# Moving weight and quantization work between engines in a gated cross-attention and ternary-FFN kernel

## The reference

```
for each of 4 batch elements (512 tokens x 512 channels):
  h    = layernorm(layernorm(x)) with weights
  q, qx, k, v = fp8(h / in_scale) @ fp8 weights        # 16, 16, 8, 8 heads of 128
  kx, vx      = ctx @ w_kv_x                            # 8 heads each
  core = softmax(LN(q)  LN(k)^T  / sqrt(128)) v         # 2 q heads per k head
  xout = softmax(LN(qx) LN(kx)^T / sqrt(128)) vx
  x1   = x + tanh(g) * ( fp8(clip([core, xout] / smooth)) @ wproj ) * scales
  a, b = int8(layernorm(x1)) @ ternary(w_gate_up)
  out  = x1 + tanh(g2) * ( int8(silu(a) * b) @ ternary(w_down) )

ternary(w) = clip(round(w / mean|w|), -1, 1) * mean|w|
```

## Time and profile before

| | us |
|---|---|
| median of 3 runs (lowest, highest) | 1862.5 (1860.2, 1867.2) |
| the profiled execution | 1860.7 |
| its span, first to last instruction | 1858.9 |
| PE busy | 1629.7 |
| DVE busy | 1575.9 |
| ACT busy | 1350.9 |
| POOL busy | 1095.2 |

### The profile page before, as it was taken

How to read it: one execution, slowest core, us unless ns; L and a number is a source line. 1 busy time by engine, 2 the same in 40 slices (tenths; PEclk the granted TensorE clock), 3 DMA queues, 4 the chain that set the end, 5 groups by cost and what they waited for, 6 DMA issues and landing times.

```text
span 1858.9 us, 35181 instructions
## 1 busy us (share of the span) xinstructions
PE 1629.7 (88%) x11164; PEld 1007.7 (54%) x11164; DVE 1575.9 (85%) x3451; ACT 1350.9 (73%) x3351; POOL 1095.2 (59%) x1421
## 2 busy tenths in 40 slices
PE   2478899788999998899899888999999879999996
PEld 1355555455656665566566555666666434444442
DVE  7569899999898899988888999999988856777774
ACT  6468998777889987898898788998988842222222
POOL 3677888876776777776777667777767530000000
PEclk9889999999999999999999999999999989999997
DMA  3357899889999998899899998999999966322200
GB/s 101 96 149 168 190 192 211 174 187 193 203 226 202 194 224 180 191 208 249 192 207 200 229 193 195 233 231 222 217 232 181 205 157 214 105 69 80 69 18 17
DMA packets 669597, 325.48 MB, mean 175 GB/s; under 512 B 552288, under 2 KB 595424, under 8 KB 669152
## 3 DMA queue, kind: packets, MB, share of 16 engines
q1 hardware_dynamic: 669408, 323.17, 77.5%
HBM read 140.61 MB, written 48.23 MB: 102 GB/s over the span
## 4 chain that ended last, share of the span: by engine, by line
PE 41%; DVE 26%; POOL 12%; ACT 8%; issue 7%; DMA 4%; SPq 1%; ACTq 0%; DVEq 0%; POOLq 0%
PE psum L699 7%; PE psum L687 6%; PE psum L654 6%; PE psum L741 6%; PE psum L716 6%; DVE pp L981 5%; DVE nmx L971 5%; PE psum L661 3%; DMA pt<-pp 3%; PE psum L758 3%; PE psum L674 2%; POOL wbt L1513 2%; POOL qk L1566 2%; ACT pp L1330 1%; POOL ars L1544 1%
## 5 line engine op out<-in xcount | busy, mean ns | idle before, releaser
L687 PE MATMUL psum<-qk 128*128 128x512 f16 x1536 | 421.9, 384 | 29.0 <-DVE pp L981 22.9
L699 PE MATMUL psum<-pt,vv 128*128 128x512 f16 x1536 | 398.5, 382 | 55.8 <-ACT cy L1338 40.6
L654 PE MATMUL psum<-wbt,xqt 128*128 128x256 f16 (+1 forms) x4096 | 411.3, 251 | 25.1 <-DVE xqt L898 11.1
L654 PEld LDWEIGHTS psum<-wbt,xqt 128*128 128x128 f16 x4096 | 333.6, 100 | 135.5 <-issue 20.4
L1319 ACT ACTIVATE psum<-psum,nmx 128x512 f32<-128x512 f32 x512 | 344.4, 673 | 84.9 <-DVE nmx L971 80.4
L981 DVE SCALAR_TENSOR_TENSOR pp<-psum,prs,pp 128x512 f16<-128x512 f32 x512 | 378.5, 739 | 5.5 <-ACT pp L1330 5.2
L971 DVE TENSOR_REDUCE nmx<-psum 128x1 f32<-128x512 f32 x512 | 344.5, 673 | 36.7 <-PE psum L687 35.2
L1330 ACT ACTIVATE pp<-psum,prs 128x512 f16<-128x512 f32 x512 | 356.7, 697 | 18.5 <-DMA pt<-pp 18.2
L699 PEld LDWEIGHTS psum<-pt,vv 128*128 128x128 f16 x1536 | 147.5, 98 | 252.5 <-issue 70.0
L1566 POOL TENSOR_TENSOR qk<-y,qk 128x512 f16<-128x512 f32 x192 | 233.7, 1217 | 16.0
L687 PEld LDWEIGHTS psum<-qk 128*128 128x128 f16 x1536 | 143.8, 99 | 114.7 <-DVE pp L981 26.0
(11 more groups left out here) (176 smaller groups left out, 2711.1 us busy)
## 6 DMA issues: line engine op xcount, KB each, us to landing
wbt<-ws SPq DMA_DIRECT2D x192, 256.0 KB, 3.8
ws<-wbt SPq DMA_DIRECT2D x64, 256.0 KB, 4.0
catd<-cy SPq DMA_DIRECT2D x64, 256.0 KB, 3.3
raw<-in_wgu SPq DMA_DIRECT2D x64, 256.0 KB, 3.6
raw<-in_w SPq DMA_DIRECT2D x32, 384.0 KB, 3.7
wbt<-catd SPq DMA_DIRECT2D x6, 2048.0 KB, 9.8
pt<-pp SPq DMA_TRANSPOSE x512, 3.7
raw<-in_wp SPq DMA_DIRECT2D x32, 256.0 KB, 3.8
```

The lines of the kernel that those rows point to most:

```text
L654: ins = e.matmul(bank[:, o0:o0 + c1 - c0], xv[:, v, kt * 512 + tt * 128:kt * 512 + (tt + 1) * 128], wb[i][:, h, kt, c0:c1], start=kt == 0 ...
L687: ins = e.matmul(SB(n), qk[i][:, jq, u, ss], qk[i][:, jk, w, :], start=k == 0, stop=k == 2)
L699: ins = e.matmul(OB, v[:, t, u, att, :], src[:, w, t, :], start=t == 0 and k == 0, stop=t == 3 and k == 2)
```

## The change

Five edits, all in phase A: (1) the high part of a split job is made by ACT (`job_hi`, at slot n, behind ACT's other work) instead of POOL; (2) its low part by POOL at n+1 instead of DVE; (3) in a ternary job POOL clips the rounded value in place at n+1, to MAGIC - 1 and MAGIC + 1, and DVE only subtracts MAGIC, at n+2; (4) for batch elements 2 and 3 the clip of each input part is done by POOL in the same slot; (5) all output steps come one slot later. In slots modulo 16 the output clip moves from 1 and 9 to 2 and 10, the DVE steps from 2, 3, 4 and 10, 11, 12 to 3, 4, 5 and 11, 12, 13, the subtractions from 5, 7, 13, 15 to 6, 8, 14, 0.

```diff
-POOL_HI = 2
+POOL_HI, POOL_X = 2, 2
-OUT_AT = {"clip": 17, "field": 18, "step": 19, "add": 20, "sub": (21, 23), "store": 26}
+OUT_AT = {"clip": 18, "field": 19, "step": 20, "add": 21, "sub": (22, 24), "store": 27}
@@ DVE x_quant
+                if step == 0 and b >= POOL_X:
+                    return
@@ DVE job
-                if what == "tern":
-                    q.done(e.tensor_scalar(ob, f, MAGIC, 1.0, ALU.subtract, ALU.min))
-                    e.tensor_scalar(ob, ob, -1.0, None, ALU.max).then_inc(s["l_t2"], 1)
-                else:
-                    e.tensor_tensor(o.bitcast(F16)[:, 0:512], f, wps[:, j, :], ALU.subtract).then_inc(s["l_lo"], 1)
+                q.wait_ge("l_tc", JV["l_tc", m])
+                e.tensor_scalar(raw[i][:, 512:768].bitcast(BF16)[:, 0:512], raw[i][:, 0:512], MAGIC, None,
+                                ALU.subtract).then_inc(s["l_t2"], 1)
-                if JOB_AT.get(n - 1, -1) >= 0:
-                    job(JOB_AT[n - 1])
+                if JOB_AT.get(n - 2, -1) >= 0:
+                    job(JOB_AT[n - 2])
@@ ACT
+            def job_hi(m):
+                j, i = JOBS[m][2], (K0 + m) % 2
+                q.wait_ge(f"raw_ld{i}", JV[f"raw_ld{i}", K0 + m])
+                e.activation(wps[:, j, :], raw[i][:, 0:512], ACT.Copy).then_inc(s["l_hi"], 1)
@@ POOL
+            def x_clip(b, k):
+                part = k // 5
+                v, half_ = divmod(part, 2)
+                src = xq[b % 2][:, v, half_ * 1024:(half_ + 1) * 1024]
+                q.wait_ge("xy", xy_value(b, 3, v))
+                q.wait_ge("x_w", ((b - 1) * 8 + part) * 4)
+                e.tensor_scalar(src, src, 448.0, -448.0, ALU.min, ALU.max).then_inc(s["x_w"], 1)
@@ POOL job (now called at n + 1)
                 if what == "split":
-                    e.tensor_scalar(wps[:, j, :], raw[i][:, 0:512], 1.0, 1.0, ALU.mult, ALU.mult).then_inc(s["l_hi"], 1)
+                    q.wait_ge("l_hi", JV["l_hi", m])
+                    e.tensor_tensor(o.bitcast(F16)[:, 0:512], f, wps[:, j, :], ALU.subtract).then_inc(s["l_lo"], 1)
+                elif what == "tern":
+                    q.wait_ge("l_t1", JV["l_t1", m])
+                    e.tensor_scalar(f, f, MAGIC + 1.0, MAGIC - 1.0, ALU.min, ALU.max).then_inc(s["l_tc"], 1)
+                for b, k in x_steps(n, "quant"):
+                    if k % 5 == 0 and b >= POOL_X:
+                        x_clip(b, k)
-                if JOB_AT.get(n, -1) >= 0:
-                    job(JOB_AT[n])
+                if JOB_AT.get(n - 1, -1) >= 0:
+                    job(JOB_AT[n - 1])
```

More of the change, by code:

```diff
@@ L186, in job_tables @@
             up("l_t1", m)
+            up("l_tc", m)
             up("l_t2", m)
@@ L271 @@
     "scores mx exp rc sc hi lo tr0 tr1 tr2 tr3 pv o_y o_c o_w o_q "
-    "l_sum l_r l_ar l_sc l_t1 l_t2 l_hi l_lo l_ab l_fr l_fa flag "
+    "l_sum l_r l_ar l_sc l_t1 l_tc l_t2 l_hi l_lo l_ab l_fr l_fa flag "
     "id_b pj x1 f_mv f_rs h1b h1_tr h1t gu sl hh hx h2m hq m3 h2_tr hqt dn fin "
@@ L998, in job @@
             def job(m):
-                what, src, j, _ = JOBS[m]
+                if JOBS[m][0] != "tern":
+                    return
                 i = (K0 + m) % 2
-                f, o = raw[i][:, 0:512], raw[i][:, 512:768]
-                if what in ("sum", "scale"):
-                    return
                 stored, summed = JB[m]
-                if what == "tern":
[L1006 to L1009, removed]
-                    q.done(e.tensor_scalar(ob, f, MAGIC, 1.0, ALU.subtract, ALU.min))
-                    e.tensor_scalar(ob, ob, -1.0, None, ALU.max).then_inc(s["l_t2"], 1)
-                else:
[L1013 to L1016, removed]
-                    e.tensor_tensor(o.bitcast(F16)[:, 0:512], f, wps[:, j, :], ALU.subtract).then_inc(s["l_lo"], 1)
+                q.wait_ge("l_tc", JV["l_tc", m])
+                q.wait_ge(f"l_st{i}", JV[f"l_st{i}", stored])
+                q.wait_ge("l_ab", JV["l_ab", summed])
+                e.tensor_scalar(raw[i][:, 512:768].bitcast(BF16)[:, 0:512], raw[i][:, 0:512], MAGIC, None,
+                                ALU.subtract).then_inc(s["l_t2"], 1)
             def weight_sums():
@@ L1420, in act_program @@
                     ctx_hi(b, kt)
+                if JOB_AT.get(n, -1) >= 0 and JOBS[JOB_AT[n]][0] == "split":
+                    job_hi(JOB_AT[n])
                 for at in (n, n - 2):
@@ L1582, in job @@
                 i = (K0 + m) % 2
+                f, o = raw[i][:, 0:512], raw[i][:, 512:768]
                 if what == "split":
-                    q.wait_ge(f"raw_ld{i}", JV[f"raw_ld{i}", K0 + m])
-                    e.tensor_scalar(wps[:, j, :], raw[i][:, 0:512], 1.0, 1.0, ALU.mult, ALU.mult).then_inc(s["l_hi"], 1)
+                    stored, summed = JB[m]
+                    q.wait_ge("l_hi", JV["l_hi", m])
+                    if stored is not None:
+                        q.wait_ge(f"l_st{i}", JV[f"l_st{i}", stored])
+                        q.wait_ge("l_ab", JV["l_ab", summed])
+                    e.tensor_tensor(o.bitcast(F16)[:, 0:512], f, wps[:, j, :], ALU.subtract).then_inc(s["l_lo"], 1)
+                elif what == "tern":
+                    q.wait_ge("l_t1", JV["l_t1", m])
+                    e.tensor_scalar(f, f, MAGIC + 1.0, MAGIC - 1.0, ALU.min, ALU.max).then_inc(s["l_tc"], 1)
             q.wait_ge("pre_v", 1)
```

## The result

The changed kernel takes 1894.8 us (median of 4 runs, 1894.0 to 1899.2) against 1862.8 for the kernel before in the same session: ratio 1.0176, 95% interval 1.0161 to 1.0192. It is 32 us slower, above the whole predicted range (1838 to 1880). The profiled execution took 1894.5, its span 1892.7, which is 33.8 more than before.

A forecast was written before the change was run, and what follows sets the result against it. Stretches were taken as PE-bound (17 of 32), DVE-bound (eight) or, in the first five, a chain of waits led by POOL. Terms: -33.7 + 20 + 3 + 4 + 2 + 3 = -1.7, giving 1859 us, range 1838 to 1880.

The forecast's parts named there:

- the ternary edit: Ternary jobs: one of two DVE operations removed, -4.9 us in DVE-bound slots; POOL's added clips, +33 of work, off the path.
- Rival 4: Input and ternary clips: DVE waits for POOL, so 8.8 + 4.9 us come back, 1872.7 us; chance 0.05.
- The output clip's wait: Slot 11: DVE's field step waits 2.3 us for POOL's clip; +7 in PE-bound, +10 in DVE-bound, +3 in first five stretches.
- the slack of 1.94 us: PE's score tile after slot 11 in a PE-bound stretch: 1.94 us of slack just covers the 1.6 us delay.
- The shift as a whole: Output steps one slot later: +20 us for DVE's wait on the output clip, +3 for subtractions moved on POOL.
- the moved subtractions: POOL's output subtractions, odd to even slots behind rstd: 0.6 us in each of five early stretches, +3 (-3 to +6).
- The splits: Output weights' low parts off DVE, -20 us (-9 to -44); high parts on ACT, +3 (0 to +10).
- The input clips: Batch elements 2 and 3: 16 clips of 552 ns off DVE, -8.8 us, all in DVE-bound stretches.
- contention: DVE-bound slots: POOL gets 30 us more work and DVE steps wait for its instructions to end, +4 us (0 to +30).
- ACT and SP: ACT's added high parts +3 us, its sum waiting for POOL in four cases; SP's later output store 0 (to +3).
- high if PE-bound stretches rise above 40.5: Sign set in advance: PE-bound stretches, expected at 39.2 to 39.7 us, rising above 40.5 mean the forecast fails high.
- Rival 1: Slot 11: the wait comes through under PE too, 1.6 us in 17 stretches, 28 instead of 7, 1880 us; chance 0.13.

The follow-up runs named there:

- e8: The changed kernel with POOL's ternary clip first in its slot, ahead of rstd and the shifted subtraction; 1879.7 us.
- e15: The changed kernel with the output subtractions one slot later still, in slots 7, 9, 15, 1; 1882.9 us.
- e14: The kernel before with only the output subtractions and the store moved one slot later; 1878.1 us.
- e3: The kernel before with edits (1) and (2) alone, high parts on ACT and low parts on POOL; 1850.8 us.
- e10: The changed kernel without edit (5), the input clips on POOL one slot earlier; 1852.0 us.
- e13: The kernel before with DVE output steps, subtractions and store one slot later, the output clip left in slots 1 and 9; 1867.1 us.
- e12: The changed kernel with POOL's ternary clip first in its slot and the output clip in front of the head; 1865.1 us.
- e9: The kernel before with edits (1), (2) and (3) alone, without input clips on POOL or later output steps; 1847.7 us.

## Why the prediction was wrong

**The step that failed** is the ternary edit: "so it stays off the path by sum", and "The remaining operation ... I take as L1010 was". POOL's sum is indeed no limit, 32.21 of 43.2 us in the ternary stretch of the fifth window. But POOL's list is in order, and edit (5) puts a subtraction of 1.15 us ahead of the ternary clip in the very slots (0, 6, 8, 14) in which POOL also waits for DVE. The prediction moved each edit by itself and never wrote POOL's new list of one slot with both in it. Rival 4 had the wait ("DVE waits for the clip") but priced it at the removed operation's 4.9; measured, DVE waits 31.4 us, and e8 and e15 give 15.2 and 11.9 back by taking it away. With -4.9 booked and about +15.5 measured by leaving (3) out, this term was off by 20 of the 36 us. Most of the rest is in the input clips and the splits, below.

**The output clip's wait** was right in mechanism and place: 2.3 us forecast in slot 11, 2.42 in the row; that stretches without jobs absorb it was right too (39.5 before, 39.6 after). The row with the slack of 1.94 us was itself read in such a stretch (slot 459) and then taken for all 17 PE-bound ones; with (5) alone the four ternary ones from 368 to 431 are 0.8 us longer on average, not 0.4. The shift as a whole had +20 and +3, and (5) alone measured +20.6. In its trace the 17 PE-bound stretches are 8.0 us longer in sum (7 forecast), the eight DVE-bound 11.3 (10), the first five 6.8 (3 and 3). But the sum is right for a partly wrong reason: e14 shows that the moved subtractions ("clip and subtraction now stand behind a wait for DVE instead of filling it"), which were put at +3, at +6 at most, and for the first five stretches alone, cost 16.4 by themselves, through the same field step. The two effects overlap; which share of the 20.6 is whose can't be given as a sum.

**The splits** had -20 on DVE and +3 on ACT, so -17, within the first bounds; measured -11.5 (-16 to -7 by the interval). The work removed was 34.6 us. The "three or four" PE-bound cases were right: in the trace of e3 the stretches from slots 112 (that of the earlier trace rows), 128, 256 and 272 are 10.0 us shorter together, for 9 forecast (the one from 448, where (1) and (2) change nothing, is 3.6 longer in the same trace). What was too large is "DVE is the bound, all of it counts": the two stretches of the earlier trace rows, from 192 and 208, are 4.7 shorter, for 8.8. L1338 took 682 ns, for which 638 was taken, and L1601 1165 for 1217.

**The input clips** had -8.8 with +2 for `spread` and a part of the +4 for contention; alone they measured +5.3 (+2.8 to +9.3 by the interval). The sign is wrong, and this term is off by some 12 us. POOL's clip takes 1091 ns where DVE's took 552. DVE waits for it 8.2 us in the kernel after, nearly the 8.8 of rival 4, but only 3.4 with (4) alone, where the +5.3 was measured, and e10 without that wait was no faster. The cause of this loss stays open; slots 208 to 239 carry 4.4 of it.

**ACT and SP.** ACT's sum (L1354) waits 6.1 us for POOL's low part, in 5 cases, where four were forecast. ACT's wait for DVE's reciprocal grew from 81.0 to 105.4 us, and PE's for ACT's `cy` from 40.6 to 52.2; by DVE's waits above that was to be expected, but no run shows it apart. What the high parts cost on ACT is not shown apart from the splits' -11.5. PE's product waits no longer for the DMA transposes than before (12.5 for 14.8), so nothing shows the store that comes later on SP to cost anything.

Of the marks set in advance, "before L991 idle time of some 50 us" came with 55.3 in slot 11, the step "near 0.45" took 0.470 (L996), and the field step "near 0.8" 0.589 (L994). In the first window with quantizing DVE's busy time fell by 4.4 us and the span by 1.8, near the 4 and "2 to 3" set for it; in the second the span grew by 2.6. L913 to L919 changed by under 0.1 us each, so that mark stayed silent. "high if PE-bound stretches rise above 40.5" is the one that fired, with 43.2 in the four ternary stretches from 368 to 431 (39.1 to 40.9 before); those from 432 and 448, where the jobs have ended, stand at 39.4 and 39.6 as before. Rival 1, slot 11 through under PE everywhere, is not what happened: with (5) alone the PE-bound stretches lost 8 us, not its 28 (17 times 1.6 is 27).

What stays open: the 5.4 us of e13 (its interval begins just above no change), in which DVE waits less than before; what the input clips cost; and why a stretch with jobs loses time to these waits where one without jobs absorbs slot 11's. In e12 17 us are still missing against e9; (4) and the shift's rest (e13) could fill some 10 of them, which no run shows.

## What to carry to other kernels

When several edits touch one in-order engine, write out its whole new list for each slot and walk it from its last wait to the instruction that another engine wants next: a sum of busy time, 75% in the ternary stretch here, says nothing about it. Moving an instruction that DVE doesn't wait for (the output subtraction) from a slot without a wait to one behind a wait delays everything after it on that engine; in this kernel that cost 16.4 us, more than the 11.5 that the removal of 34.6 us of DVE work brought. Measure the edits alone and left out: three of five together were worth 15 us, 11.5 by the splits alone, and that was hidden beneath two that cost more.

## What the runs showed of the hardware

How long a DVE instruction takes depends on what POOL is doing when it starts: the same subtraction (128x512 float32 to bfloat16) took 432 ns on average in the kernel after, 572 in e15 and 682 in e8, which differ only in the place of instructions in POOL's list. In e8 it took 416 ns in 18 cases, and 819 in the 23 that started during a POOL subtraction of 1.16 us, which all ended 0.28 us after that subtraction. The same in-place clip of 128x1024 bfloat16 took 552 ns on average on DVE and 1091 on POOL; the float32 clip of 128x512 took 692 on POOL. The low part took 1083 on DVE (676 at the least) and 1165 on POOL. The Trainium skill (GPSIMD Engine Reference, Engine selection) would leave such elementwise work on VectorE, as about twice as slow with two inputs; by the 676 ns at the least on DVE the trace agrees (1165 on POOL is 1.7 times that), but beside POOL's other work the two engines were nearly equal here, and e9, with low parts and ternary clips on POOL, is 15 us faster than before.
